# Recurrent layers: where the sums over states of items 8 to 11 and the heads' first addition stand in the order

## The chip, the cores and the metric

The kernel runs on one NeuronCore of one Trainium2 chip. The metric is the device time of one execution in microseconds (us). The kernel before takes 3003.28 us, the median of three runs (2997.95 to 3004.85).

## The reference

Four layers run one after the other on x of 16 sequences, 100 tokens and 512 features, all in float32. Layers 0 and 2 are cross-attention layers, and the change does not touch them. Layers 1 and 3 are recurrent blocks (RWKV) with 32 heads of 16 features. Cut to what matters, with `ln` for layer normalisation:

```python
xa = ln(x); sx = previous_token(xa) - xa
xxx = einsum('blfd,fde->blfe', tanh((xa + sx*maa_x) @ maa_w1).reshape(b, l, 5, 32), maa_w2)
xk, xw, xv, xr, xg = (xa + sx * (maa_stack[j] + xxx[j]) for j in range(5))
w = exp(-exp(time_decay + tanh(xw @ td_w1) @ td_w2))
r, k, v, g = xr @ Wr.T, xk @ Wk.T, xv @ Wv.T, silu(xg @ Wg.T)
# for every token, with a state s of 16 x 16 per head
a = k_t[..., :, None] * v_t[..., None, :]
out = einsum('bhi,bhij->bhj', r_t, u * a + s)
s = a + w_t[..., :, None] * s
x1 = x + (head_norm(out) * g) @ Wo.T
xc = ln(x1); sx2 = previous_token(xc) - xc
y = x1 + sigmoid((xc + sx2*ffn_maa_r) @ Wfr.T) * (square(relu((xc + sx2*ffn_maa_k) @ Wfk.T)) @ Wfv.T)
```

## The kernel before, in words

**Groups and turns.** Each recurrent layer works on eight groups of two sequences (200 tokens, 512 features as four chunks of 128 partitions). A turn of its loop handles three stages at once: the recurrence of group i (`rec`), the front of group f = i + 1 (`front`: first norm, the five mixed inputs, and the first halves of k, v and r), and the back of group b = i - 1 with the feed-forward tail of group i - 2 (`back`, `tail`). In this document, turn 0 is the first with a recurrence. Turns 0 and 1 are written out, turns 2 to 6 are a hardware loop, turn 7 has no front, and further turns drain. Turns 1 to 6 have both front and back and are called middle turns. Each engine runs the turns through an order written out by hand, and the engines meet at semaphores only.

**The recurrence.** The state is cut into 16 items per group. For item n, VectorE (DVE) makes `product(n)` (line 740: k times the spread v, two inputs in SBUF, output in PSUM) and `scan(n)` (line 755: the recurrence over tokens, into buffer n % 4 of a ring). GpSimd (POOL) multiplies the scanned states by r in place (line 1164), which it starts only after `kv` n + 2, the product of item n + 1. TensorE (PE) then sums a pair of items over the states: `reduce(p)` (line 521, eight matmuls) handles items 2p and 2p + 1. So `reduce(4)` needs POOL's items 8 and 9, and `reduce(5)` needs items 10 and 11. `scan(n)` for n of 4 and more waits for the reduce that frees its buffer: `scan(12)` waits for `reduce(4)`, `scan(14)` for `reduce(5)`.

**The half of the heads.** `reduce(0)` to `reduce(3)` fill PSUM bank 6 with the first half of the heads. DVE adds that bank to `bon` (line 902, signal `head_out`), and `reduce(4)` overwrites the bank, so it waits for `head_out`.

**The front around the change.** PE computes `mix(x)` (line 544, eight matmuls on 32 rows), DVE turns its result into `mix_term(x)` (line 763), and POOL adds the token (`add_token`, line 1144, signal `mixed`). On POOL, `add_token(2)` stands before its item 10, and `add_token(3)` before its item 11, both in the same queue. With `mixed` 3 PE starts the first half of v (`project_half`, line 530, 16 matmuls), and with `mixed` 4 the first half of r. Between them it makes the decay (line 695), which waits for `mix_term(3)`, since both use banks 4 and 5. `mix(4)` follows r, and then comes the feed-forward projection fk (line 530, 32 matmuls).

**The back around the change.** DVE multiplies the second norm by its reciprocal deviation (`m.n2.scale`, line 270, two inputs in SBUF). ScalarE (ACT) makes `xc` of it (line 1096), and DVE subtracts neighbours after `scan(12)` (line 915, two inputs in SBUF) and mixes them (line 921).

Of the kernel before, what the change touches and what calls it, by code (L numbers as in the profile page):

```python
# [313 lines left out]
def project(pe, core, w, weight, src, k_chunks=C, m_chunks=range(C)):  # L314
# [20 lines left out]
    head_out=2, head_mean=1, head_centred=1, head_squares=1, head_var=1, head_log_var=1, head_rstd=1,  # L335
# [62 lines left out]
def rwkv(core, m, name, base, after):  # L398
# [7 lines left out]
    def wait(eng, n, i, k=0):  # L406

        eng.wait_ge(m.s[n].sem, m.s[n].at(i, k))

    def sem(n):  # L410
        return m.s[n].sem
# [12 lines left out]
    def rows(v, cc):  # L424

        return v[:, 2 * cc:2 * cc + 2].rearrange("p c b e -> p (c b) e")

    def half(v, h):

        return v[:, 2 * h:2 * h + 2, :].rearrange("p c n -> p (c n)")  # L430

    def full(b):

        return psum[:, b, 0:2 * N]

    def chunk(b, j, a=0, z=P):

        return psum[a:z, b, j * N:(j + 1) * N]

    def item(n):  # L440

        cc, q, odd = n // 8, n % 8 // 2, n % 2
        return cc, q, 8 * odd + q, 2 * odd
# [35 lines left out]
    def rest(n, eng, k, front, rec):  # L479

        if front and not rec and after.tail:
            after.tail[n](eng, k)
# [26 lines left out]
    def tensor(pe):  # L509
        def body(i, g, front, rec, back, tail):  # L510
            f, b, t = i + 1, i - 1, i - 2

            def reduce(pair, j):

                wait(pe, "r_states", j, 2 * pair + 2)
                for n in (2 * pair, 2 * pair + 1):
                    cc, q, _, t0 = item(n)
                    rv = m.ring[n % 4].rearrange("p (h c) (b e) -> p h (c b) e", h=2, b=NB)
                    for h in range(2):
                        r0 = 32 * (t0 + h)  # L520
                        mm = pe.matmul(psum[r0:r0 + 32, 6, 0:2 * N], core.red_w[:, 24 - 8 * q:56 - 8 * q],  # L521
                                       rv[:, h, :, 0:L], start=q == 0, stop=q == 3)
                mm.then_inc(sem("r_states_sum"), 1)

            def project_half(n, src, h, bank, told):

                for j in range(2):
                    for k in range(C):
                        c = 2 * h + j
                        mm = pe.matmul(chunk(bank, j), m.W[n][:, k, c * P:(c + 1) * P], src[:, k, :], start=k == 0,  # L530
                                       stop=k == C - 1)
                mm.then_inc(sem(told), 1)
# [7 lines left out]
            def mix(x):  # L540

                w, th, r0 = (m.w2, m.tha, DM * x) if x < 4 else (m.low, m.thl, BACK)
                for c in range(C):
                    mm = pe.matmul(chunk(4 + c // 2, c % 2), w[r0:r0 + DM, c * P:(c + 1) * P], th[r0:r0 + DM, :],  # L544
                                   start=True, stop=True)
                mm.then_inc(sem("mix_sum"), 1)
# [128 lines left out]
            if front:  # L675
                wait(pe, "mixed", f, 2)
                rest(0, pe, "bank 3 read", front, rec)
                for k in range(C):
                    mm = pe.matmul(chunk(3, 0, 0, DD), m.td1[:, k, :], m.xm[1][:, k, :], start=k == 0, stop=k == C - 1)
                mm.then_inc(sem("decay_hidden_sum"), 1)  # L680

                wait(pe, "mix_term", f, 12)
                mix(3)
                wait(pe, "mixed", f, 3)
                wait(pe, "k", f, 1)
                project_half("v", m.xm[2], 0, 2, "v_sum")

            if rec:
                wait(pe, "head_out", i, 1)
                reduce(4, i)  # L690
            if front:
                wait(pe, "decay_hidden", f, 1)
                wait(pe, "mix_term", f, 16)
                for c in range(C):
                    mm = pe.matmul(chunk(4 + c // 2, c % 2), m.low[0:DD, c * P:(c + 1) * P], m.thl[0:DD, :], start=True,
                                   stop=True)
                mm.then_inc(sem("decay_sum"), 1)
                wait(pe, "mixed", f, 4)
                project_half("r", m.xm[3], 0, 3, "r_sum")

                wait(pe, "decay_rate", f, 4)
                mix(4)

            if rec:
                reduce(5, i)
            if back:
                wait(pe, "ffn_mix", b, 4)
                if front:
# [4 lines left out]
                project_half("fk", m.xk2, 1, 3, "ffn_k_sum")  # L713

        turns(pe, body)


    def vector(dve):
        def body(i, g, front, rec, back, tail):
            f, b, t = i + 1, i - 1, i - 2  # L720

            def step(n):

                product(n)
                scan(n)

            def product(n):

                if not rec:
                    return  # L730
                cc, _, _, _ = item(n)
                if n % 8 == 0:
                    wait(dve, "k", i, cc + 1)
                wait(dve, "starts", i, n + 1)
                if n:
                    wait(dve, "states", i, n)
                elif back:
                    wait(dve, "states", b, 16)
                kb = rows(m.k, cc).rearrange("p a e -> p (a e)").unsqueeze(1).broadcast_to([P, 2, 4 * E])
                dve.tensor_tensor(m.kv.rearrange("p (h x) -> p h x", h=2), kb,  # L740
                                  m.spread[n % 4].rearrange("p h a e -> p h (a e)"), ALU.mult).then_inc(sem("kv"), 1)

            def scan(n):

                if not rec:
                    return
                cc, _, _, _ = item(n)
                wait(dve, "kv", i, n + 1)
                if n >= 4:
                    wait(dve, "r_states_sum", i, (n - 4) // 2 + 1)  # L750
                elif back:
                    wait(dve, "r_states_sum", b, n // 2 + 7)
                if n % 8 == 0:
                    wait(dve, "decay", i, 2 * cc + 2)
                dve.tensor_tensor_scan(m.ring[n % 4].rearrange("p j e -> p (j e)"),  # L755
                                       m.we[:, cc].rearrange("p j e -> p (j e)"), m.kv, 0.0,
                                       ALU.mult, ALU.add).then_inc(sem("states"), 1)

            def mix_term(x):

                wait(dve, "mix_sum", f, x + 1)
                for c in range(C):
                    dve.scalar_tensor_tensor(m.xm[x][:, c, :], chunk(4 + c // 2, c % 2), vec(f"stack{x}", c),  # L763
                                             m.sx[:, c, :], ALU.add, ALU.mult).then_inc(sem("mix_term"), 1)
# [128 lines left out]
                mix_term(2)  # L893
                rest(1, dve, "scale 3", front, rec)

            step(11)
            if back:
                m.n2.scale(dve, b)
            if rec:
                wait(dve, "r_states_sum", i, 4)  # L900
                wait(dve, "bonus", i, 1)
                dve.tensor_tensor(half(m.bon, 0), full(6), half(m.bon, 0), ALU.add).then_inc(sem("head_out"), 1)
            if front:
                if rec:
                    wait(dve, "r_sum", i, 2)
                mix_term(3)
                if not rec and after.tail:
                    dve.wait_ge(*after.done)
                    columns()
# [28 lines left out]
        def columns():  # L938

            dve.memset(m.we.rearrange("p c j (b e) -> p (c j b) e", b=NB)[:, :, 0:1], 0.0).then_inc(sem("columns"), 1)  # L940
            dve.memset(m.k.rearrange("p c b e -> p (c b) e")[:, :, 0:1], 1.0).then_inc(sem("columns"), 1)
            dve.memset(m.v.rearrange("p c b e -> p (c b) e")[:, :, 0:1], 0.0).then_inc(sem("columns"), 1)

        if not after.tail:
            core.wait_before(dve, after)
            wait(dve, "weights", occ + 1)
            columns()
        turns(dve, body)


# [1582 lines left out]
```

## Time and profile before

| what | value |
|---|---|
| median of three runs | 3003.28 us |
| the profiled execution, its own time | 3000.84 us |
| its span, first to last instruction | 2999.0 us |
| PE matmuls busy | 2781.7 us (93%) |
| DVE busy | 2018.5 us (67%) |
| ACT busy | 1338.5 us (45%) |
| POOL busy | 665.4 us (22%) |
| mean granted TensorE clock | 0.97 |

Busy time is a share of the whole span, the attention layers too. The recurrent layers take the stretches from about 640 to 1240 us and from about 2330 to 2930 us. In the timeline a row gives the start, the duration, engine, line and operation; a bracket at its end is the idle time of that engine just before, and what ended it. Rows of matmuls under each other overlap a little, since matmuls are pipelined.

### The profile page before, as it was taken

What the parts mean: (1) busy time and instruction counts of PE and PEld (TensorE: products, weight loads), DVE (VectorE), ACT (ScalarE), POOL (GpSimd) and SP (SyncE); (2) the same over time, 40 slices, a digit from 0 to 9 for tenths busy, and PEclk for the clock granted to TensorE, in tenths of its full rate; (3) what the DMA queues carried; (4) which work ended last, traced back from release to release, by engine and by line L of the source; (5) the groups of instructions that cost most, each with busy time, mean ns of one, the idle gap of its engine ahead of it and who ended that gap; (6) DMA issues with size and microseconds to landing.
All of it is one profiled execution on the core that took longest, in us unless ns stands there. A gap on an engine that the chain in (4) does not pass through costs nothing.

```text
span 2999.0 us, 53538 instructions
## 1 busy us (share of the span) xinstructions
PE 2781.7 (93%) x18016; PEld 2164.3 (72%) x18016; DVE 2018.5 (67%) x4921; ACT 1338.5 (45%) x3438; POOL 665.4 (22%) x436
## 2 busy tenths in 40 slices
PE   7999999988999999789999999999999799999986
PEld 7555555766888888685445554899999678888876
DVE  2878787678999999654555555511101899999992
ACT  1888888543444443353444444332311244444432
POOL 0010101034444444200000000000000544444440
PEclk9999999988999999899999999999999899999998
DMA  2101010323333223300000000210001433333340
GB/s 109 37 24 35 24 35 13 134 75 98 90 93 89 86 85 94 101 28 20 21 20 30 20 20 10 113 64 23 0 0 51 119 90 92 89 89 88 91 127 11
DMA packets 96168, 182.86 MB, mean 61 GB/s; under 512 B 10250, under 2 KB 87626, under 8 KB 92334
## 3 DMA queue, kind: packets, MB, share of 16 engines
q1 hardware_dynamic: 96046, 181.27, 19.3%
q8 instruction: 72, 1.18, 0.2%
q14 instruction: 50, 0.41, 0.0%
HBM read 171.34 MB, written 9.90 MB: 60 GB/s over the span
## 4 chain that ended last, share of the span: by engine, by line
PE 67%; DVE 12%; issue 10%; ACT 7%; POOL 1%; DMA 1%; DVEq 0%; SPq 0%; ACTq 0%; POOLq 0%
PE psum L530 20%; PE psum L318 10%; PE psum L2005 6%; PE psum L1892 4%; PE psum L1363 3%; DVE psum L740 3%; PE psum L521 3%; ACT arena L1648 3%; ACT arena L2257 2%; PE psum L1905 2%; PE psum L1947 2%; PE psum L537 2%; PE psum L1375 2%; DVE arena L755 2%; PE psum L544 2%
## 5 line engine op out<-in xcount | busy, mean ns | idle before, releaser
L530 PEld LDWEIGHTS psum<-arena 128*128 128x128 f32 x4096 | 720.3, 197 | 135.1 <-issue 79.6
L530 PE MATMUL psum<-arena 128*128 128x200 f32 x4096 | 770.4, 346 | 50.6 <-DVE arena L921 18.6
L1164 POOL TENSOR_TENSOR arena<-arena 128x800 f32<-128x800 f32 x256 | 454.5, 1778 | 453.2 <-DVE psum L740 453.2
L755 DVE TENSOR_TENSOR_SCAN arena<-arena,psum 128x808 f32<-128x808 f32 x256 | 470.0, 1836 | 37.4 <-PE psum L521 22.1
L318 PE MATMUL psum<-arena 128*128 128x200 f32 (+1 forms) x1920 | 332.3, 335 | 15.1 <-POOLq L140 13.4
L318 PEld LDWEIGHTS psum<-arena 128*128 128x128 f32 x1920 | 327.9, 191 | 16.9 <-POOLq L140 13.3
L1648 ACT ACTIVATE arena<-arena 100x361 f32<-100x361 f32 x512 | 300.5, 590 | 87.4 <-DVE arena L1575 85.8
L1144 POOL TENSOR_TENSOR arena<-arena 128x800 f32<-128x800 f32 x80 | 141.4, 1767 | 741.6 <-DVE arena L763 499.1
L1575 DVE CUSTOM_DVE_ANT_0 arena<-psum,arena 100x361 f32<-100x361 f32 x512 | 254.2, 530 | 45.4 <-ACT arena L1648 37.8
L740 DVE TENSOR_TENSOR psum<-arena 128x808 f32<-128x808 f32 x256 | 280.5, 1096 | 5.5
L1363 PEld LDWEIGHTS psum<-arena 100*128 100x128 f32 x1536 | 146.3, 142 | 131.2 <-ACT arena L1660 60.3
L2257 ACT ACTIVATE arena<-arena 100x361 f32<-100x361 f32 x256 | 149.6, 587 | 146.3 <-DVE arena L2141 146.3
L1363 PE MATMUL psum<-arena 100*128 100x100 f32 x1536 | 189.5, 258 | 24.1 <-ACT arena L1660 23.9
L1947 PEld LDWEIGHTS psum<-arena 100*128 100x128 f32 x768 | 84.5, 141 | 148.5 <-issue 74.6
L1905 PE MATMUL psum<-arena 128*128 128x512 f32 (+1 forms) x384 | 189.4, 605 | 0.0
L1892 PE MATMUL psum<-arena 128*128 128x361 f32 x512 | 180.3, 477 | 1.6 <-DVE arena L2073 1.5
L2005 PE MATMUL psum<-arena 128*128 128x200 f32 x1024 | 174.9, 333 | 0.0
L2005 PEld LDWEIGHTS psum<-arena 128*128 128x128 f32 x1024 | 173.4, 190 | 0.1
L964 ACT ACTIVATE arena<-arena 128x8 f32 (+1 forms) x256 | 54.0, 212 | 266.4 <-DMA arena<-v_rows 265.1
L521 PE MATMUL psum<-arena 128*32 128x400 f32 x1024 | 127.5, 537 | 23.6 <-POOL arena L1164 14.2
L544 PE MATMUL psum<-arena 32*128 32x200 f32 x640 | 135.2, 352 | 13.9 <-DVE arena L763 7.5
L2127 DVE COPY arena<-psum 128x300 f32<-128x300 f32 x128 | 59.8, 467 | 130.4 <-PE psum L1947 130.4
(143 smaller groups left out, 3833.3 us busy)
## 6 DMA issues: line engine op xcount, KB each, us to landing
arena<-v_rows SPq DMA_DIRECT2D x512, 202.0 KB, 3.2
arena<-ctxT SPq DMA_DIRECT2D x32, 722.0 KB, 4.2
arena<-L_w SPq DMA_DIRECT2D x10, 1024.0 KB, 7.9
arena<-L_w SPq DMA_DIRECT2D x8, 1152.0 KB, 16.1
v_rows<-arena SPq DMA_DIRECT2D x32, 202.0 KB, 2.0
arena<-L_fc SPq DMA_DIRECT2D x4, 1024.0 KB, 7.9
arena<-L_pj SPq DMA_DIRECT2D x4, 1024.0 KB, 15.8
arena<-xT SPq DMA_DIRECT2D x4, 800.0 KB, 12.0
```

Source lines behind the costliest of these rows:

```text
L318: mm = pe.matmul(core.part(w, m), weight[:, k, m * P:(m + 1) * P], src(k), start=k == 0, stop=k == k_chunks - 1)
L521: mm = pe.matmul(psum[r0:r0 + 32, 6, 0:2 * N], core.red_w[:, 24 - 8 * q:56 - 8 * q], rv[:, h, :, 0:L], start=q == 0, stop=q == 3)
L530: mm = pe.matmul(chunk(bank, j), m.W[n][:, k, c * P:(c + 1) * P], src[:, k, :], start=k == 0, stop=k == C - 1)
L740: dve.tensor_tensor(m.kv.rearrange("p (h x) -> p h x", h=2), kb, m.spread[n % 4].rearrange("p h a e -> p h (a e)"), ALU.mult).then_inc(sem ...
L755: dve.tensor_tensor_scan(m.ring[n % 4].rearrange("p j e -> p (j e)"), m.we[:, cc].rearrange("p j e -> p (j e)"), m.kv, 0.0, ALU.mult, ALU. ...
L1164: pool.tensor_tensor(sv, sv, rb, ALU.mult).then_inc(sem("r_states"), 1)
L1363: mm = pe.transpose(bank[4 + 3 * (n % 2)][:, j * L:(j + 1) * L], pr[h % 8][0:L, j * P:(j + 1) * P], ident[0:L, 0:L])
L1575: dve.tensor_tensor_reduce(out=sm[n][0:L], in0=bank[n][0:L, 0:S], in1=nmask[u][0:L], scale=1.0, scalar=FLT, op0=ALU.add, op1=ALU.min, accu ...
L1648: act.activation(pr[k % 8][0:L, 0:S], sm[n][0:L], ACT.Exp, bias=nmx[0:L, k:k + 1], scale=-1.0, accum_out=den[0:L, k:k + 1]).then_inc(exp_r ...
L1892: mm = pe.matmul(bank[6 + c % 2][:, 0:S], Wk[:, k, c * P:(c + 1) * P], ctxt[u % 2][:, k, :], start=k == 0, stop=k == C - 1)
L1905: mm = pe.matmul(bank[6 + j % 2][0:n, :], ctxt[u % 2][:, k, a:a + n], Wv[:, k, :], start=k == 0, stop=k == C - 1)
L2005: mm = pe.matmul(part(2 + q % 2, m), fc[:, k, j * P:(j + 1) * P], norms[u].yc[:, k, :], start=k == 0, stop=k == C - 1)
```

## The change: what it does

On PE, in turns with a front, `reduce(4)` and its wait for `head_out` move ahead of the first half of v, and `reduce(5)` moves from behind `mix(4)` to between the decay and the first half of r. On DVE, the addition that signals `head_out` moves from behind `scan(11)` and the second norm's scaling to between `product(11)` and `scan(11)`. No instruction is added or removed, and no DMA is moved. The queues of ACT, POOL and SP keep their order.

```diff
@@ tensor
                 mix(3)
-                wait(pe, "mixed", f, 3)
-                wait(pe, "k", f, 1)
-                project_half("v", m.xm[2], 0, 2, "v_sum")
-
             if rec:
                 wait(pe, "head_out", i, 1)
                 reduce(4, i)
             if front:
+                wait(pe, "mixed", f, 3)
+                wait(pe, "k", f, 1)
+                project_half("v", m.xm[2], 0, 2, "v_sum")
+
                 wait(pe, "decay_hidden", f, 1)
                 wait(pe, "mix_term", f, 16)
...
                 mm.then_inc(sem("decay_sum"), 1)
+            if rec:
+                reduce(5, i)
+            if front:
                 wait(pe, "mixed", f, 4)
                 project_half("r", m.xm[3], 0, 3, "r_sum")

                 wait(pe, "decay_rate", f, 4)
                 mix(4)

-            if rec:
-                reduce(5, i)
@@ vector
-            step(11)
-            if back:
-                m.n2.scale(dve, b)
+            product(11)
             if rec:
                 wait(dve, "r_states_sum", i, 4)
                 wait(dve, "bonus", i, 1)
                 dve.tensor_tensor(half(m.bon, 0), full(6), half(m.bon, 0), ALU.add).then_inc(sem("head_out"), 1)
+            scan(11)
+            if back:
+                m.n2.scale(dve, b)
```

## Rows read from the trace of the kernel before

**Rows 1.** The page, part 1: busy time and share of the span

```profile
PE 2781.7 (93%) x18016; PEld 2164.3 (72%) x18016; DVE 2018.5 (67%) x4921; ACT 1338.5 (45%) x3438; POOL 665.4 (22%) x436
```

**Rows 2.** Windows of two turns; the number behind POOL's is the granted clock

```profile
841.10:918.61 77.51, 75.76 (x449) 64.65 (x449) 74.38 (x89) 32.35 (x68) 37.13 (x22) 1.00 0.33 91
918.61:997.00 78.39, 77.02 (x448) 66.35 (x449) 73.22 (x89) 32.35 (x68) 37.14 (x22) 0.98 0.31 90
```

**Rows 3.** The chain that ended last, in order of time: start, duration, what

```profile
916.75 1.74 POOL arena L1144
...
918.61 4.63 PE psum L530 x16
```

**Rows 4.** Timeline of PE in the turn with the full clock

```profile
838.35 1.62 PE L544 MATMUL psum<-arena 32*128 32x200 f32 x8
841.10 2.97 PE L530 MATMUL psum<-arena 128*128 128x200 f32 x16 [1.14 <-POOL arena L1144]
844.00 0.88 PE L521 MATMUL psum<-arena 128*32 128x400 f32 x8
844.80 1.62 PE L695 MATMUL psum<-arena 64*128 64x200 f32 x8
846.51 2.98 PE L530 MATMUL psum<-arena 128*128 128x200 f32 x16
...
851.77 5.68 PE L530 MATMUL psum<-arena 128*128 128x200 f32 x32
```

**Rows 5.** Timeline of DVE in the same stretch

```profile
839.11 1.84 DVE L755 TENSOR_TENSOR_SCAN arena<-arena,psum 128x808 f32<-128x808 f32 x1
840.87 0.97 DVE L270 TENSOR_TENSOR arena<-arena 128x800 f32<-128x800 f32 x1
841.75 0.57 DVE L902 TENSOR_TENSOR arena<-psum,arena 128x400 f32<-128x400 f32 x1
842.23 1.42 DVE L763 SCALAR_TENSOR_TENSOR arena<-psum,arena 128x200 f32<-128x200 f32 x4
843.57 1.00 DVE L740 TENSOR_TENSOR psum<-arena 128x808 f32<-128x808 f32 x1
844.94 1.84 DVE L755 TENSOR_TENSOR_SCAN arena<-arena,psum 128x808 f32<-128x808 f32 x1 [0.38 <-PE psum L521]
846.70 2.30 DVE L915 TENSOR_TENSOR arena<-arena 128x800 f32<-128x800 f32 x1
...
853.18 1.40 DVE L763 SCALAR_TENSOR_TENSOR arena<-psum,arena 128x200 f32<-128x200 f32 x4
```

**Rows 6.** Timeline of POOL in the same stretch

```profile
839.24 1.73 POOL L1144 TENSOR_TENSOR arena<-arena 128x800 f32<-128x800 f32 x1 [1.02 <-DVE psum L740]
840.92 2.51 POOL L1164 TENSOR_TENSOR arena<-arena 128x800 f32<-128x800 f32 x1
844.72 1.74 POOL L1144 TENSOR_TENSOR arena<-arena 128x800 f32<-128x800 f32 x1 [1.29 <-DVE psum L740]
846.42 1.74 POOL L1164 TENSOR_TENSOR arena<-arena 128x800 f32<-128x800 f32 x1
```

**Rows 7.** Timeline of PE at the same place one turn later

```profile
918.61 4.63 PE L530 MATMUL psum<-arena 128*128 128x200 f32 x16 [1.14 <-POOL arena L1144]
...
925.53 2.97 PE L530 MATMUL psum<-arena 128*128 128x200 f32 x16
...
930.79 5.68 PE L530 MATMUL psum<-arena 128*128 128x200 f32 x32
```

**Rows 8.** Timeline of DVE in that turn, at scan 12

```profile
924.12 1.84 DVE L755 TENSOR_TENSOR_SCAN arena<-arena,psum 128x808 f32<-128x808 f32 x1 [2.04 <-PE psum L521]
```

**Rows 9.** Timeline of all engines in turn 0

```profile
695.02 1.73 POOL L1164 TENSOR_TENSOR arena<-arena 128x800 f32<-128x800 f32 x1
695.77 2.97 PE L530 MATMUL psum<-arena 128*128 128x200 f32 x16
```

**Rows 10.** Timeline of all engines in turn 7, at scan 12

```profile
1225.06 1.84 DVE L755 TENSOR_TENSOR_SCAN arena<-arena,psum 128x808 f32<-128x808 f32 x1 [0.84 <-PE psum L521]
```

## The prediction

> **What bounds the kernel now.** The page comes first [rows 1]: over the whole span PE is 93% busy and DVE 67%, but this mixes attention layers with recurrent ones. So I cut the recurrent part into turns, from one first half of v to the next [rows 2]. A turn with the full clock lasts 77.51 us, with PE busy 75.76 and DVE 74.38: both are nearly full. The next turn has a granted clock of 0.98 and lasts 78.39 us. Windows over all turns show the pattern twice: per layer the middle turns 1 and 2 have the full clock at the v projection, and turns 3 to 6 the low one, eight low places in all.
>
> The chain of waits says who leads [rows 3]. It comes down DVE, goes through POOL's `add_token(2)` and then enters PE at the v projection, and from there it stays on PE until the next turn's out projection. A delay of PE behind this place is therefore a delay of the turn. The timelines of PE, DVE and POOL around this place [rows 4 to 6] carry the sum. Their times are those of the turn with the full clock, and the changed kernel's are given on the same scale.
>
> At the low clock the same 16 matmuls take 4.63 us instead of 2.97 [rows 4, 7]. That is 1.66 us, at 1.2 instead of 2.4 GHz by the granted clock of that stretch, and PE had stood idle 1.14 us just before. The fk projection then starts 930.79 - 851.77 = 79.02 us after its predecessor, 1.51 more than 77.51 [rows 4, 7], yet the turn grows by 0.88 only [rows 2]. So 0.63 us of a PE delay is absorbed later in the turn.
>
> **Part 1: `reduce(4)` ahead of v.** `mix(3)` ends at 838.35 + 1.62 = 839.97, and v starts at 841.10 [rows 4]. `reduce(4)` takes 0.81 from its start to the next matmul (844.00 to 844.80), so it fits into this idle time, if `head_out` is there. With DVE's addition directly behind `product(11)`, which has ended when `scan(11)` starts at 839.11, it ends near 839.6. So v starts when it did, the 0.81 behind v is free, and `scan(12)` no longer waits 0.38 us [rows 5], or 2.04 at the low clock [rows 8]. What is late next is `mix_term(3)`, for which the decay waits, and after it everything in part 3.
>
> **Part 2: the addition ahead of `scan(11)`.** It costs DVE nothing net, since it only moves: from its start to the next instruction is 842.23 - 841.75 = 0.48 us. But it makes `scan(11)` and the scaling behind it later by some 0.4 us, and this loses a race. Two rows show what the race is worth. The scaling (line 270) starts at 840.87, POOL's item 10 at 840.92: DVE is first, takes 0.97, and POOL takes 2.51 instead of 1.74 [rows 5, 6]. At 846.70 DVE's subtraction (line 915), of the same shape, starts after POOL's item 11 (846.42) and takes 2.30, ending at 849.00, 0.84 behind POOL's end at 848.16. Whoever has two SBUF inputs and comes second waits for the first. After the change the scaling is issued at about 841.3, behind POOL's 840.92. It waits for POOL's end at 840.92 + 1.74 = 842.66 and ends at 843.50, not 841.84: +1.66. The addition is no longer behind it (-0.48), so `mix_term(3)` and `product(12)` are late by 1.18 us. ACT's `xc`, which needs the scaling, is late by 1.66 as well; its four activations still have 4 us between 843.50 and the issue of line 915, which needs them, near 847.5. ACT evicts v behind it, some 1.3 us later than now; fk, which waits for that, is later still, and so is SP's store of v rows.
>
> **Part 3: `reduce(5)` ahead of r.** Its condition is POOL's item 11, which stands behind `add_token(3)` and so behind `product(12)`. POOL reaches it at 846.42 + 1.18 = 847.60. There the same race comes again: `scan(12)` without its wait ends one DVE step earlier, so line 915 is issued 1.79 us after `product(12)` ends (0.03 to the scan, 1.76 in it) and POOL's item 11 starts 1.85 after (846.42 - 844.57) [rows 5, 6]. That is the spacing of line 270 and item 10 today, where DVE wins by 0.05. So item 11 takes 2.51 and ends at 850.11. PE's `reduce(5)` starts 0.13 later, as v does behind `add_token(2)` [rows 4, 6], at 850.24, and r at 851.05 instead of 846.51: +4.54. `mix(4)` moves with it. fk has `reduce(5)` no longer just before it (-0.81): +3.73 us. PE stands idle about 3.7 us between the decay, which ends near 846.5, and 850.24, where it stands almost none now. Queued behind this wait are r, `mix(4)` and fk; DVE's `mix_term(4)` waits for `mix(4)` and moves from 853.18 [rows 5] to about 855.6, 2.4 us, which is less than PE's delay, so PE stays the bound.
>
> **The clock.** Four of six middle turns pay 0.88 now; filled idle time ahead of v should end that (-3.5 per layer). But an idle time of 1.14 brings the low clock in four turns of six, and the new one is three times as long. I take it to fall in each of six turns. The row's price is 1.66 [rows 4, 7], with no slack left to absorb any; bounds are 0, if it stays, and 2.9, if the low clock lasts nearly twice as long. I take 1.4, near the row, since part of the slow stretch may lie on idle time.
>
> **Turns 0 and 7.** In turn 0 POOL's item 11 ends at 696.75; `reduce(5)` then delays r from 695.77 to about 697.7 [rows 9], and `product(13)` would now start just ahead of POOL's item and stretch it by 0.77: +2.6 us, from +1.1 to +3. In turn 7 there is no front: `head_out` comes earlier, `scan(12)` loses its wait of 0.84 [rows 10]: -0.8.
>
> **The sum.** A middle turn: 77.51 + 3.73 - 0.63 + 1.4 = 82.0 us. Per layer 6 x (3.73 - 0.63 + 1.4) = 27.0, less 3.5, plus 2.6, less 0.8: +25.3. Two layers: +50.6 us. The profiled execution took 3000.84 us, 1.84 more than its span and 2.4 less than the median; added to the median of 3003.28 the sum gives 3054 us.
>
> A rule bears on one uncertain step. No row shows what happens if line 921, right behind 915 on DVE and also with two SBUF inputs, competes with the waiting POOL. The Trainium skill, "SBUF — State Buffer", section "Who interferes with whom", says that the order of issue decides and that the second one waits until the first has finished; POOL, waiting since 847.60, would go ahead of line 921. By that rule the sum stays at +50.6, and the third rival below is unlikely. The races of part 2 agree with it.
>
> **Rivals.**
> - No race is lost, only the wait for item 11 remains (the addition shifts DVE less than the 0.05 us that decide). r starts at 848.16 + 0.13 + 0.81 = 849.10, fk is late by 2.59 - 0.81 = 1.78, a turn by 1.15 + 1.4. Per layer 15.3 - 3.5 + 1.9 - 0.8 = 12.9: 3029 us. Against it: 0.4 is much more than 0.05.
> - The clock doesn't fall in the new idle time: 6 x 3.1 - 3.5 + 1.8 per layer, +34: 3037 us. With the first rival it would be 6 x 1.15 - 3.5 + 1.1, +9: 3012 us.
> - POOL's item 11 has to wait for lines 915, 921 and `product(13)` in a row, 2.5 us more per turn: some 3084 us.
> - No change: the low clock stays on the v projection, and in its shadow the wait for item 11 costs little; per layer within 3 us, 3003 to 3009. This speaks against part 1, where the idle time ahead of v goes.
> - Faster: `reduce(5)` is never late and only gains remain, 8 low clocks of 0.88 and 2 x 0.8 from turn 7: 3003.3 - 8.6 = 2994.7 us. The place is PE behind the decay; it decides if POOL has item 11 ready by about 846.5, when now it ends at 848.16 even at best. DVE would have to be 1.7 us earlier at `product(12)`, and nothing ahead of that product gets faster.
>
> **How the numbers follow.** A measurement of this kernel can tell about 0.2% (6 us) from no change. The forecast, with one or both races lost and a low clock, has 0.6 (3035 to 3070). First rival 0.08, second 0.1, the third 0.06, no change 0.09, faster 0.07. The forecast and rivals one to three are slower by over 0.2%: 0.84. The range runs from 3012, where the race and the clock both spare the kernel, to 3084, the third rival.
>
> **What the profile would show.** Right: `reduce(4)` (line 521) directly behind `mix(3)`, no idle time ahead of `scan(12)`; line 270 in middle turns at about 2.2 us; POOL's item 10 at 1.74 and item 11 at about 2.5; PE idle some 3.7 us ahead of `reduce(5)`, ended by POOL line 1164; the low clock behind this; turns near 82 us; the chain running DVE 270, 763, 740, POOL 1144, 1164, PE 521. Wrong: line 270 still at 0.97 (first rival), turns of 77 us (faster), or a low clock still at v (no change).

## The result, and the profile after

The changed kernel takes 3052.48 us, the median of four runs (3051.62 to 3056.06). Against 3004.07 us for the kernel before, over its runs beside and before these, the ratio is 1.0162 with a 95% interval of 1.0149 to 1.0175: slower by 48 us. The prediction was 3054 us, in a range of 3012 to 3084.

From the first heads' addition of a recurrent layer to that of its turn 7 the first of them takes 559.9 us instead of 532.4, the second 560.3 instead of 535.3 (starts of lines 902 and 901 in the timelines). That is 52.6 us together, against 51.1 in the span, so the whole loss lies where the change is. Lines behind the edited place have new numbers: product 741, scan 756, mix_term 764, the addition 901, the subtraction 917, the second norm's mixing 923, POOL's token 1146 and item 1166. Each run's rows carry the line numbers of its own kernel.

The page of the changed kernel, its span, part 1 and the row of the sums over states in part 5:

```profile
span 3050.1 us, 53538 instructions
PE 2790.3 (91%) x18016; PEld 2165.7 (71%) x18016; DVE 2050.4 (67%) x4921; ACT 1336.4 (44%) x3438; POOL 662.2 (22%) x436
L521 PE MATMUL psum<-arena 128*32 128x400 f32 x1024 | 135.7, 570 | 68.0 <-POOL arena L1166 65.1
```

PE is busy 8.6 us more than in [rows 1] for the same matmuls, which is the clock, and it stands idle 68.0 us ahead of the sums, 65.1 of them for POOL's items. In the kernel before this was 23.6 us on the page. Windows of middle turns 1 to 3 of the first layer, from one v projection to the next, to compare with [rows 2]:

```profile
765.74:849.19 83.45, 78.31 (x448) 66.88 (x449) 75.99 (x89) 32.20 (x68) 37.24 (x22) 0.96 0.31 85
849.19:931.91 82.72, 77.58 (x449) 66.13 (x449) 75.95 (x89) 32.12 (x68) 37.23 (x22) 0.96 0.31 85
931.91:1013.79 81.88, 77.59 (x449) 66.15 (x449) 76.16 (x89) 32.20 (x68) 36.37 (x22) 0.96 0.31 87
```

The granted clock is 0.96 in each of them. From v to v the ten measurable middle turns of both layers last 81.9 to 83.7 us, instead of 77.5 or 78.4. Cutting a turn at the start of fk shows where the time is lost. The first three windows are of the kernel before: v to fk and fk to the next v in the turn with the full clock, then fk to the next v in one with the low clock on v. The last two are of the changed kernel, v to fk and fk to the next v:

```profile
841.10:851.77 10.67, 10.58 (x65) 8.25 (x65) 10.22 (x15) 5.56 (x15) 6.06 (x4) 1.00 0.31 92
851.77:918.61 66.84, 65.18 (x389) 56.39 (x385) 64.16 (x75) 26.79 (x53) 31.07 (x19) 1.00 0.34 91
930.79:997.00 66.21, 64.84 (x388) 56.42 (x385) 63.16 (x75) 26.90 (x53) 29.88 (x19) 1.00 0.32 92
849.19:865.68 16.49, 11.92 (x56) 9.54 (x56) 12.94 (x15) 5.31 (x16) 7.58 (x4) 0.79 0.27 83
865.68:931.91 66.23, 65.66 (x394) 56.59 (x393) 63.01 (x74) 26.81 (x54) 29.65 (x18) 1.00 0.31 86
```

Behind fk nothing is lost: 66.2 us, as in the late turns of the kernel before. The whole loss lies between v and fk, 16.49 us instead of 10.67. The timeline of PE in the changed kernel, at the place of [rows 4]:

```profile
847.98 0.88 PE L521 MATMUL psum<-arena 128*32 128x400 f32 x8
849.19 2.97 PE L530 MATMUL psum<-arena 128*128 128x200 f32 x16 [0.33 <-POOL arena L1146]
853.00 1.62 PE L695 MATMUL psum<-arena 64*128 64x200 f32 x8 [0.84 <-DVE arena L764]
858.35 1.56 PE L521 MATMUL psum<-arena 128*32 128x400 f32 x8 [3.73 <-POOL arena L1166]
859.84 4.37 PE L530 MATMUL psum<-arena 128*128 128x200 f32 x16
864.14 1.61 PE L544 MATMUL psum<-arena 32*128 32x200 f32 x8
```

The sum of items 8 and 9 sits where PE was idle, and v runs at the full clock (2.97). The decay now waits 0.84 us for `mix_term(3)`. Then PE waits 3.73 us for POOL's item 11, and the sum and r behind it run at the low clock: 1.56 and 4.37 us instead of 0.88 and 2.98. DVE there, to hold against [rows 5]:

```profile
845.89 1.27 DVE L741 TENSOR_TENSOR psum<-arena 128x808 f32<-128x808 f32 x1
847.08 0.56 DVE L901 TENSOR_TENSOR arena<-psum,arena 128x400 f32<-128x400 f32 x1
847.56 1.82 DVE L756 TENSOR_TENSOR_SCAN arena<-arena,psum 128x808 f32<-128x808 f32 x1
849.31 2.30 DVE L270 TENSOR_TENSOR arena<-arena 128x800 f32<-128x800 f32 x1
851.53 1.41 DVE L764 SCALAR_TENSOR_TENSOR arena<-psum,arena 128x200 f32<-128x200 f32 x4
852.87 0.99 DVE L741 TENSOR_TENSOR psum<-arena 128x808 f32<-128x808 f32 x1
...
855.74 0.97 DVE L917 TENSOR_TENSOR arena<-arena 128x800 f32<-128x800 f32 x1
856.74 2.79 DVE L923 SCALAR_TENSOR_TENSOR arena<-arena 128x200 f32<-128x200 f32 x4
...
865.79 1.43 DVE L764 SCALAR_TENSOR_TENSOR arena<-psum,arena 128x200 f32<-128x200 f32 x4 [3.47 <-PE psum L544]
```

And POOL, to hold against [rows 6]:

```profile
849.02 1.74 POOL L1166 TENSOR_TENSOR arena<-arena 128x800 f32<-128x800 f32 x1
854.02 1.73 POOL L1146 TENSOR_TENSOR arena<-arena 128x800 f32<-128x800 f32 x1 [3.26 <-DVE psum L741]
855.71 2.58 POOL L1166 TENSOR_TENSOR arena<-arena 128x800 f32<-128x800 f32 x1
```

Both races stand in these rows. In the first one, between DVE's scaling and POOL's item 10, item 10 starts at 849.02 and the scaling at 849.31, so POOL takes 1.74 and the scaling 2.30. The second one is between DVE's subtraction and POOL's item 11. The starts of DVE's subtraction (855.74) and POOL's item 11 (855.71) lie 0.03 us apart in the records, too close to tell who was first; the durations tell it: DVE takes 0.97 and POOL 2.58. The chain of waits of the changed kernel shows the path, times as before:

```profile
849.31 0.14 DVE arena L270
849.44 2.09 issue
851.53 1.41 DVE arena L764 x4
...
854.02 1.73 POOL arena L1146
855.75 2.55 POOL arena L1166
...
858.35 1.56 PE psum L521 x8
```

### The profile page after: what moved, and what is told of

Same layout as the page of the kernel before. It is cut to its first block, busy times and chain, and to the rows that moved or that the text cites. A ratio compares the mean times of both kernels' runs of the same rounds, so it can differ in the third digit from the quotient of the medians.

```text
span 3050.1 us, 53538 instructions
## 1 busy us (share of the span) xinstructions
PE 2790.3 (91%) x18016; PEld 2165.7 (71%) x18016; DVE 2050.4 (67%) x4921; ACT 1336.4 (44%) x3438; POOL 662.2 (22%) x436
## 3 DMA queue, kind: packets, MB, share of 16 engines
q8 instruction: 72, 1.18, 0.2%
## 4 chain that ended last, share of the span: by engine, by line
PE 66%; DVE 13%; issue 10%; ACT 7%; POOL 2%; DMA 1%; DVEq 0%; ACTq 0%; SPq 0%; POOLq 0%
PE psum L530 20%; PE psum L318 10%; PE psum L2007 6%; PE psum L1894 4%; PE psum L1365 3%; DVE psum L741 3%; PE psum L521 3%; ACT arena L1650 3%; ACT arena L2259 2%; DVE arena L756 2%; PE psum L1907 2%; PE psum L1949 2%; PE psum L544 2%; PE psum L537 2%; DVE arena L764 2%
## 5 line engine op out<-in xcount | busy, mean ns | idle before, releaser
L521 PE MATMUL psum<-arena 128*32 128x400 f32 x1024 | 135.7, 570 | 68.0 <-POOL arena L1166 65.1
L764 DVE SCALAR_TENSOR_TENSOR arena<-psum,arena 128x200 f32<-128x200 f32 x320 | 113.0, 414 | 81.5 <-PE psum L544 81.5
```

## Experiments

### The sum of items 10 and 11 back behind mix 4

```diff
-            if rec:
-                reduce(5, i)
-            if front:
                 wait(pe, "mixed", f, 4)
...
                 mix(4)
 
+            if rec:
+                reduce(5, i)
```

> The changed kernel with the sum of items 10 and 11 back behind mix 4; the sum of items 8 and 9 ahead of v and the heads' addition between product and scan 11 stay. Theory (what costs is the sum of 10 and 11 waiting for POOL's item 11 in front of r): r then waits only for POOL's token 3, about 1.2 us later than in the kernel before because the scaling (line 270) still loses its race (2.3 us instead of 0.97). PE's idle time of 2.9 to 3.7 us ahead of that sum is gone, a middle turn is 78.1 us at the full clock and up to 79.5 with a low clock: 3003 us without low clocks, 3014 with one in each turn. Rival (the move of the sum of 8 and 9 or of the addition carries the loss): stays above 3035 us.

Measured: 3006.57 us, ratio 1.001 (0.9997 to 1.0022). PE's timeline in a middle turn:

```profile
925.65 2.97 PE L530 MATMUL psum<-arena 128*128 128x200 f32 x16 [0.33 <-POOL arena L1145]
929.46 1.62 PE L695 MATMUL psum<-arena 64*128 64x200 f32 x8 [0.84 <-DVE arena L763]
932.26 2.97 PE L530 MATMUL psum<-arena 128*128 128x200 f32 x16 [1.19 <-POOL arena L1145]
```

One move on PE carries 46 of the 48 us. No middle turn has a low clock any more. Still a turn lasts 78.3 to 78.8 us, not the 78.1 of the expectation: the scaling and the subtraction are both stretched in most turns (2.3 and 2.6 us), and DVE is as busy as PE there (75.9 and 75.8 us of a turn).

### The heads' addition ahead of product 11, the rest of the change kept

```diff
-            product(11)
             if rec:
                 wait(dve, "r_states_sum", i, 4)
...
+            product(11)
             scan(11)
```

> The changed kernel with the heads' addition ahead of product 11 instead of between product and scan 11. Product 11 waits for POOL's item 9 there anyway, so it should end only 0.2 us later; scan 11 follows it directly and the scaling is issued ahead of POOL's item 10 again: line 270 at 0.97, POOL's item 10 at 2.5. Theory (two lost races plus the wait for item 11): mix_term 3 and product 12 come about 1.4 us earlier than in the changed kernel, the sum of 10 and 11 too; a middle turn near 80.6 us and 3037 us in all, 3028 if POOL wins the second race. Rival (the race of the scaling costs nothing, since PE waits for POOL anyway): 3050 us or more.

Measured: 3046.55 us, ratio 1.0135 (1.0111 to 1.016), well above the 3037 expected, below the 3050 of the rival. DVE and then POOL:

```profile
924.84 0.57 DVE L900 TENSOR_TENSOR arena<-psum,arena 128x400 f32<-128x400 f32 x1
925.32 1.00 DVE L741 TENSOR_TENSOR psum<-arena 128x808 f32<-128x808 f32 x1
...
928.11 0.97 DVE L270 TENSOR_TENSOR arena<-arena 128x800 f32<-128x800 f32 x1
```

```profile
928.17 2.50 POOL L1166 TENSOR_TENSOR arena<-arena 128x800 f32<-128x800 f32 x1
...
933.40 2.58 POOL L1166 TENSOR_TENSOR arena<-arena 128x800 f32<-128x800 f32 x1
```

The first race is won again as expected: with 1.00 instead of 1.27 for product 11, the scaling at 0.97, item 10 at 2.50. PE's idle time ahead of the sum is still 3.17 us, or 2.33 where POOL wins the second race, three times in twelve. The turns are 81.0 to 82.2 us, about 1 us shorter than in the changed kernel where DVE wins the second race in both. Part of the time gained in front of the low clock is lost in it: r behind the sum takes 5.00 us in this turn, against 4.37 in the row of the changed kernel above. Over the twelve middle turns the sum and r together take 2.5 us more than at the full clock, where my expectation had kept 1.4; and from fk to the next v pass 66.4 us instead of 66.2.

### Only the addition moved, PE's order as before

```diff
@@ vector, on the kernel before
-            step(11)
-            if back:
-                m.n2.scale(dve, b)
+            product(11)
             if rec:
...
+            scan(11)
+            if back:
+                m.n2.scale(dve, b)
```

> The kernel before with the addition moved between product and scan 11 on DVE, PE's order as before. The scaling loses its race (2.3 us). Theory: the price of that race is paid only where something waits for mix_term 3 or POOL's token 3: in turns with the full clock r starts up to 1.2 us later, in turns whose v projection runs at the low clock nothing is seen; turn 7 gains up to 0.8. 3002 to 3007 us. Rival (the race costs 1.2 us in each of 12 middle turns whatever PE does): 3017 us.

Measured: 3011.74 us, ratio 1.0023 (1.0012 to 1.0033), between theory and rival. Windows of two middle turns, one in either recurrent layer:

```profile
925.43:1003.95 78.52, 75.84 (x449) 64.66 (x449) 75.67 (x89) 32.13 (x68) 37.26 (x22) 1.00 0.31 90
2622.24:2701.00 78.76, 77.33 (x449) 66.07 (x449) 75.19 (x89) 32.17 (x68) 36.41 (x22) 0.98 0.32 89
```

The lost race costs even a turn with the low clock on v: 78.76 against 78.39 in [rows 2]. I had priced it at nothing there. From v to fk such a turn takes 12.16 us, as before (12.18); the loss lies behind fk, 66.60 instead of 66.21, where DVE has more to do than before. In the first layer v keeps the full clock in each middle turn, with 1.14 us of idle time ahead of it in turns 2 to 6, and the turn is long nonetheless, since r waits 1.19 us for POOL's token. Four middle turns have a low clock where the kernel before has eight, so this run's total shows the race's price less what those four turns give back.

### Only the sum of items 10 and 11 moved

```diff
@@ tensor, on the kernel before
                 mm.then_inc(sem("decay_sum"), 1)
+            if rec:
+                reduce(5, i)
+            if front:
                 wait(pe, "mixed", f, 4)
...
-            if rec:
-                reduce(5, i)
```

> The kernel before with only the sum of items 10 and 11 moved ahead of r; the sum of 8 and 9 stays behind v, the addition stays behind the scaling. No race is newly lost: line 270 at 0.97. The sum starts behind POOL's item 11, 1.8 us later fk in a full-clock turn, 0.2 in one whose v runs at the low clock; the new idle time ahead of the sum is near 1.9 us and may bring a low clock of its own. Theory: 3010 us (no new low clocks) to 3027 (one in each middle turn), with 3020 as the value. Rival (the move of the sum alone carries the whole loss): 3045 us or more.

Measured: 3015.44 us, ratio 1.0036 (1.0022 to 1.005), inside the theory's range and well below its value. Three successive turns show all three cases, the full clock, the low clock behind the new wait, and the low clock on v:

```profile
2624.98:2703.76 78.78, 75.43 (x448) 64.69 (x449) 74.85 (x90) 32.39 (x68) 37.33 (x23) 1.00 0.33 90
2703.76:2784.07 80.31, 77.12 (x449) 66.38 (x449) 74.70 (x89) 32.31 (x68) 37.18 (x22) 0.98 0.31 87
2784.07:2862.67 78.60, 77.07 (x448) 66.32 (x449) 73.32 (x89) 32.43 (x68) 37.14 (x22) 0.98 0.32 89
```

The first window opens 0.18 us ahead of its v; from v to v that turn lasts 78.6 us. PE waits 1.78 us for item 11 in it. There the move costs 1.1 us a turn, as the prediction's first rival had it (1.15). The two turns with the low clock behind the new wait last 80.3 us. In the six with the low clock on v the move costs 0.2 us (78.6 against 78.4). Alone this move costs 10 us, and putting it back gains 46. The rest comes from the lost races that make item 11 later, and from the low clock that comes behind the longer idle time.

### The idle time filled with matmuls

```diff
                 mm.then_inc(sem("decay_sum"), 1)
+                if rec and back:
+                    for _ in range(16):
+                        pe.matmul(chunk(7, 1), core.mean_w, m.xm[2][:, 0, :], start=True, stop=True)
             if rec:
                 reduce(5, i)
```

> The changed kernel with 16 more matmuls of 128x128 by 128x200 in each middle turn, between the decay and the sum of items 10 and 11, into half of a PSUM bank that nothing reads afterwards. Their results are not used. They take about 2.8 us, which is what PE stands idle there. Theory (the low clock behind the idle time costs about 1.3 to 1.7 us a turn): the low clock behind the sum is gone, the sum and r run at the full clock, a middle turn is 80.6 us and the whole 3033 to 3038 us although PE does 192 matmuls more. Rival (the low clock costs nothing, because PE is ahead or behind anyway): 3052 us.

Measured: 3060.2 us, ratio 1.0189 (1.0175 to 1.0204). The low clock was gone, but I had miscounted: a call in float32 stands in the trace as two matmuls, so the filling took 5.68 us and was itself in the way. A turn had the full clock and 82.44 us. This run settles nothing about the price, so it was run again with `range(8)`.

> As the run with the filled idle time, with 8 calls instead of 16. There each call stood in the trace as two matmuls, so that the filling took 5.6 us and the sum of items 10 and 11 began 1.73 us after POOL's item 11 was ready (942.45 against about 940.72). With 8 calls it takes 2.8 us and fits. Theory: the low clock stays away, a middle turn is 82.47 - 1.73 = 80.7 us, the whole near 3038 us, some 14 us below the changed kernel, which is the low clock's part of the loss. Rival (the clock is no part of it): 3052 us.

Measured: 3033.33 us, ratio 1.0093 (1.0076 to 1.0111). The timeline of PE, then windows of two of its middle turns:

```profile
932.96 1.62 PE L695 MATMUL psum<-arena 64*128 64x200 f32 x8 [0.84 <-DVE arena L767]
934.51 2.98 PE L700 MATMUL psum<-arena 128*128 128x200 f32 x16
938.31 0.88 PE L521 MATMUL psum<-arena 128*32 128x400 f32 x8 [0.83 <-POOL arena L1169]
939.12 2.97 PE L530 MATMUL psum<-arena 128*128 128x200 f32 x16
```

```profile
848.50:929.15 80.65, 78.40 (x464) 67.35 (x465) 75.95 (x89) 32.29 (x68) 37.21 (x22) 1.00 0.32 88
1009.78:1089.59 79.81, 78.39 (x464) 67.35 (x465) 76.22 (x89) 32.23 (x68) 36.38 (x22) 1.00 0.31 88
```

With more work PE is faster, by 19 us in the whole. The clock is thus about 40% of the loss. (POOL wins the second race in five middle turns of this run and in four of the changed kernel's profile, which is 0.84 us of the difference.) The first window is a turn in which DVE wins the second race, the second one in which POOL wins it: that race is worth 0.84 us.

### Both moves mended: only the sum of items 8 and 9 ahead of v stays

The diff is the first two of these experiments together.

> The changed kernel with both mendings: the sum of items 10 and 11 back behind mix 4, and the heads' addition ahead of product 11. What stays of the change is the sum of items 8 and 9 ahead of v. The scaling is issued ahead of POOL's item 10 (0.97 us), PE's idle time ahead of v shrinks to about 0.5 us, and no low clock is expected in middle turns. Theory: a middle turn near 77.5 us in all twelve instead of 77.5 in four and 78.4 in eight; 2997 us, below the kernel before. Rival (DVE bounds the turn, and product 11's 0.2 us later end and POOL's stretched item 11 cost as much as the clock gives): 3003 to 3006 us.

Measured: 2992.45 us, ratio 0.9958 (0.9946 to 0.9971), 12 us below the kernel before and better than expected. A window of a middle turn, then PE at its v projection:

```profile
1073.10:1150.56 77.46, 75.77 (x448) 64.64 (x449) 74.57 (x89) 32.35 (x68) 37.09 (x22) 1.00 0.33 91
```

```profile
1071.68 0.88 PE L521 MATMUL psum<-arena 128*32 128x400 f32 x8
1073.10 2.97 PE L530 MATMUL psum<-arena 128*128 128x200 f32 x16 [0.54 <-POOL arena L1145]
```

One of twelve middle turns has a low clock, where the kernel before has eight.

### Only the addition ahead of product 11

```diff
@@ vector, on the kernel before
+            if rec:
+                wait(dve, "r_states_sum", i, 4)
...
             step(11)
             if back:
                 m.n2.scale(dve, b)
-            if rec:
-                wait(dve, "r_states_sum", i, 4)
...
```

> The kernel before with only the heads' addition moved ahead of product 11; PE's order as before. Tells what in the repaired version gives the 12 us below the kernel before. If it is the sum of items 8 and 9 ahead of v, which fills PE's idle time there and keeps the clock up, this run shows idle time of 1.1 us or more ahead of v, low clocks in v, and 2999 to 3005 us. Rival (DVE's order alone gives it, since product 11 waits for POOL's item 9 anyway and mix_term 3 comes 0.3 us earlier): 2992 to 2996 us with the idle time and low clocks as before.

Measured: 3007.84 us, ratio 1.0013 (1.0003 to 1.0024), a little above the range expected. PE at the v projection:

```profile
1000.36 4.65 PE L530 MATMUL psum<-arena 128*128 128x200 f32 x16 [1.34 <-POOL arena L1144]
```

The idle time and the low clocks are as before (eight middle turns). DVE's order alone gives nothing; with the sum of items 8 and 9 ahead of v the time is 15 us less. So that part of the change is good, and it wants the addition ahead of the product: with the addition between product and scan the kernel took 3006.57 us, in the first experiment. What it gives with DVE's order left as it was before was not run; the addition starts there at 841.75 [rows 5], behind the idle time that the sum is to fill.

## Why the prediction was right

**`reduce(4)` ahead of v** was right: it fits the idle time, leaves 0.33 us, and ends the low clock on v and the wait of `scan(12)` in all twelve middle turns. In turn 7 the time from `product(11)` to `scan(12)` falls from 6.00 to 5.06 us, -0.94 where -0.8 was forecast.

**The addition between product and scan.** The scaling takes 2.30 as forecast, and from the end of `product(11)` to that of `product(12)` pass 6.70 us (847.16 to 853.86). Before it was 5.49 (from 837.81 + 1.27 in the timeline to 844.57 in [rows 5]): +1.21, forecast 1.18. The experiment that wins this race back shows the scaling at 0.97.

**`reduce(5)` ahead of r.** With v set to the prediction's time (841.10 for 849.19), the sum starts at 850.26; forecast was 850.24. Forecast were 3.7 us of idle time, measured 3.73 where DVE is first in the second race (3.58 in turn 1). The forecast took DVE to win always. It wins 8 of 12; in the other four POOL is first, item 11 takes 1.74, the subtraction 2.56, and PE waits 2.89. A margin of 0.05 us is no margin to count on. The turn without a low clock was forecast at 77.51 + 3.73 - 0.63 = 80.61, and the half-filled run has 80.65. That 0.63 us is absorbed stands in the windows above: 66.84 behind fk in the full-clock turn before, 66.23 in the changed kernel. DVE's `mix_term(4)` moved by 4.5 us (857.70 on that scale, from 853.18), not by 2.4, since the forecast left the clock out there; PE stayed the bound all the same, as forecast.

**The clock** is the term that was mis-sized. I took 1.4 us a turn, near the row's 1.66. Between the changed kernel and the half-filled run the two layers differ by 11.3 and 11.6 us from turn 0 to turn 7, 1.9 us for each of 12 middle turns. PE's own rows say the same: the sum and r take 2.05 us more than at the full clock, on average over the twelve. The low clock covers the sum (1.56 instead of 0.88) and most of r (4.37 instead of 2.97), and `mix(4)` behind them is at the full clock again. Over twelve turns this term was some 6 to 8 us too small. The second races that POOL won give back 4 x 0.84 = 3.4, and turn 0 was some 4 us too large. The errors have opposite signs, and so the sum came out 1.5 us from the median (+50.6 forecast, +48.4 measured): that close an agreement is luck. The same mis-sizing, in the same direction, made the expectation for the second experiment miss by 10 us.

**Turn 0** was forecast at +2.6. From its addition to turn 1's pass 76.2 us instead of 74.0 in the first layer, but 75.3 instead of 76.5 in the second, where other low clocks differ: +2.3 and -1.2, 1.0 us together where 5.2 were forecast. One part of it failed: `product(13)` did not start ahead of POOL's item 11 and stretch it by 0.77, since POOL was first (693.88 against 694.03) and took 1.73, the product 2.45. The rest is not confirmed by itself.

**The rule on ports.** It had decided against the third rival. Right behind the subtraction DVE's line 923, with two SBUF inputs, takes 2.79 us in a turn where POOL's item 11 was waiting, and 1.44 in the next turn, where it was not. POOL, waiting since before line 923 was issued, went first, as the Trainium skill says in "SBUF — State Buffer", section "Who interferes with whom". The trace agrees with it: item 11 took 2.58, not 5.

**Rivals.** The first two came out near partial kernels rather than as the result. The first was not run as it stands, with the sum of items 8 and 9 ahead of v and no race lost. With only the sum of items 10 and 11 moved the kernel takes 3015 us, not 3029: eight middle turns have a low clock, no more than before, and not twelve, and in the six with it on v the new wait costs 0.2 us. With the clock kept, 3033 was measured against 3037. The faster rival needed item 11 ready at the end of the decay, and it came 2.9 to 3.7 us later.

## What to carry to other kernels

In this kernel a wait that fitted into idle time was free, and it even kept the clock up; the same kind of wait, set where its data came 3.7 us later, cost most of its length (3.1 us of the turn) plus the clock behind it (2 us). Before moving a small VectorE operation, look which operations with two SBUF inputs stand a few hundredths of a microsecond ahead of a GpSimd operation: 0.4 us of delay turned there into 1.2 us on the path. Undo each move of a change separately: here two of three were wrong in place, and the third, with the addition set elsewhere, beats both kernels.

## What was not expected of the hardware

The low clock does not follow from the idle time alone. In the run with only the addition moved, v starts behind 1.14 us of idle time in middle turns 2 to 6 of the first layer and keeps the full clock, and behind 1.15 us in the second layer it runs at the low one (2.97 against 4.61 us). The kernel before has both with 1.14 us, one turn apart [rows 4, 7]. Nor does its price follow from the idle time: behind the same 3.7 us in the second layer of the changed kernel r takes between 3.68 and 5.32 us, and from turn 2 on the turns fall from 83.7 to 82.2 us one after the other. What decides this stays open; no run tried it.
